# Routers by maxima of eight, late norms and paired heads in stage 2, C products on VectorE or GpSimd, and one new order of an eight-stage network

## The reference, cut to what matters

```
0  L0_attn  LN, in_proj, 2 convs, silu, dt/B/C, softplus, 16-state scan over 256 steps, gate, LN, MLP
1  L0_ffn   RMS, attention (16 heads), RMS, 7 routed experts (sigmoid, top 2) + 1 shared
2  L1_attn  linear attention, 4 heads of 64, a prefix sum over 512 tokens
3  L1_ffn   MLP with binarized weights
4  L2_attn  causal attention, 16 heads over 128 columns
5  L2_ffn   8 experts, top 2 of the logits, softmax of the two, gelu
6  L3_attn  causal attention, 16 heads of 64, keys pruned by a ranking
7  L3_ffn   8 experts, softmax, top 2, weights over their sum + 1e-20, + 2 shared
```

```
scan:     h = dA_t * h + dBu_t ; y_t[d] = sum_n h[d, n] * C_t[n]
stage 2:  p = elu(x) + 1 ; q, k = p / (norm(p) + 1e-6)
          y = (q . cumsum(k v^T)) / (q . cumsum(k) + 1e-6)
routers:  scores, idx = top_k(probs, 2) ; weights dense over the experts
```

## Time and profile before

| | |
|---|---|
| runs | 1410.33, 1411.71, 1419.28 us; median 1411.71 |
| profiled execution, first to last instruction | 1417.1 us |
| PE busy | 1334.4 us (94%), 8752 records |
| PEld busy | 930.4 us (66%) |
| DVE busy | 1016.5 us (72%), 3744 instructions |
| ACT busy | 899.3 us (63%), 2493 |
| POOL busy | 711.3 us (50%), 707 |
| mean granted clock | 0.950 |
| DMA | 65.8 MB, mean 46 GB/s |

### The profile page before, as it was taken

The page is one execution under the profiler, slowest core; times in us unless marked ns, Lnnn a source line. Parts: engine busy times, 40 slices in busy tenths (PEclk is TensorE's granted clock), DMA queues, the critical chain, the costliest instruction groups (busy, mean ns, idle before and its releaser), DMA issues. The chain is left out here.

```text
span 1417.1 us, 26200 instructions
## 1 busy us (share of the span) xinstructions
PE 1334.4 (94%) x8752; PEld 930.4 (66%) x8752; DVE 1016.5 (72%) x3744; ACT 899.3 (63%) x2493; POOL 711.3 (50%) x707
## 2 busy tenths in 40 slices
PE   8778789999969999999999999999999999999997
PEld 4224455667535687677777777777888877776665
DVE  5989889794687556758687874393598998745334
ACT  6636888876633676775877776466577668744231
POOL 2736475864462655455365554638343425432543
PEclk9668999998987979999999999999999999999999
DMA  8541000001150100110010002210200002003330
GB/s 281 157 118 30 1 2 30 25 2 54 29 150 1 66 2 1 54 63 1 1 61 2 1 2 73 110 60 1 79 2 2 1 2 90 2 1 90 90 97 23
DMA packets 21278, 65.80 MB, mean 46 GB/s; under 512 B 1852, under 2 KB 8252, under 8 KB 18840
## 3 DMA queue, kind: packets, MB, share of 16 engines
q1 hardware_dynamic: 21144, 64.12, 14.2%
HBM read 61.83 MB, written 2.29 MB: 45 GB/s over the span
## 5 line engine op out<-in xcount | busy, mean ns | idle before, releaser
L1371 ACT ACTIVATE arena<-arena 128x256 f32<-128x256 f32 (+3 forms) x792 | 347.5, 442 | 52.7 <-DVE arena L1858 27.2
L1371 ACT ACTIVATE arena<-bank 128x512 f32<-128x512 f32 (+3 forms) x365 | 198.0, 570 | 258.4 <-PE bank L923 132.5
L923 PE MATMUL bank<-XT,W 128*128 128x512 f32 (+1 forms) x752 | 292.6, 524 | 0.0
L2224 POOL TENSOR_TENSOR arena<-arena 128x256 f32<-128x256 f32 x192 | 119.1, 620 | 305.8 <-DVE arena L1873 305.4
L923 PEld LDWEIGHTS bank<-W,arena 128*128 128x128 f32 x1888 | 231.9, 194 | 48.7 <-issue 38.1
L923 PE MATMUL bank<-arena 128*32 128x128 f32 (+8 forms) x2912 | 247.4, 342 | 8.5 <-DVE arena L1879 2.7
L923 PE MATMUL bank<-W,arena 128*128 128x128 f32 (+1 forms) x1888 | 244.5, 280 | 6.7 <-DVE arena L1623 3.2
L2180 POOL TENSOR_TENSOR arena<-arena 128x512 f32<-128x512 f32 (+1 forms) x108 | 171.0, 1604 | 151.6 <-DVE arena L1617 90.7
L923 PEld LDWEIGHTS bank<-arena 128*32 128x32 f32 (+4 forms) x2912 | 165.4, 157 | 89.9 <-issue 57.7
L923 PE MATMUL bank<-arena,W 128*128 128x512 f32 (+3 forms) x412 | 183.7, 684 | 25.6 <-DVE arena L1794 13.3
L927 PE MATMUL bank<-CF,arena 128*128 128x128 f32 x1312 | 186.7, 282 | 21.3 <-POOL arena L2225 6.5
(11 more groups left out here) (128 smaller groups left out, 1697.9 us busy)
## 6 DMA issues: line engine op xcount, KB each, us to landing
arena<-rws SPq DMA_DIRECT2D x8, 2048.0 KB, 7.6
arena<-rep SPq DMA_DIRECT2D x62, 256.0 KB, 5.0
arena<-rws SPq DMA_DIRECT2D x4, 1792.0 KB, 6.6
W<-w SPq DMA_DIRECT2D x2, 2124.0 KB, 8.1
arena<-rws SPq DMA_DIRECT2D x8, 384.0 KB, 10.3
W<-w SPq DMA_DIRECT2D x1, 2692.0 KB, 10.1
W<-w SPq DMA_DIRECT2D x1, 2256.5 KB, 9.0
W<-w SPq DMA_DIRECT2D x1, 2002.5 KB, 16.1
```

The lines of the kernel that those rows point to most:

```text
L923: return e.matmul(o, lhsT, rhs, start=start, stop=stop, skip_group_check=True)
L1371: return e.activation(o, a, func, **kw)
L2224: e.tensor_tensor(px[:, :, 0:128], px[:, :, 0:128], rec[:, :, 0:1].to_broadcast([128, 2, 128]), ALU.mult)
```

## The change

- **C products** leave the scan. `0.bc` now also copies C from its bank to SBUF (ACT), so that bank is free at once. A new step `0.hc` (64 of them) multiplies the scanned 128x512 by it on whichever of DVE and POOL the planner picks: 32 come to DVE, 32 to POOL. `0.ac` waits for four of them.
- **Stage 2, late norms.** exp(min(x, 0)) is made by ACT in two operations, Relu(-x) and Exp(-that), so DVE keeps one operation of 512 columns per `2.t` where it had three. q and k are transposed without the norm. A new step `2.r` makes the norms beside it: k's goes into v and its 65th column (POOL, 4x64 columns), q's multiplies the 1e-6 in `2.y`.
- **Stage 2, pairs.** `2.h` makes two heads at once, one on partitions 0 to 63 and one on 64 to 127, into two banks: 16 pairs in place of 32 single heads.
- **Routers.** Eight columns everywhere (7 + one of -1). The top two come from DVE's maximum of eight (`e.max`) and `match_replace`, each four times per router on 8 columns. Weights lie at strides of 32 columns, so stages 1 and 7 need one full transpose (128 columns) instead of four narrow ones; stage 5 has four full ones. `ew` of stages 1 and 7 is four small DMAs instead of one.
- **4.ex**: the 128 small operations go from DVE to POOL.
- **6.s** reads all 128 partitions; those of 64 up are scaled to zero in q (`half`), so it is a full matmul.
- **The planner** knows the array's division of each step (`TILED`), adds 0.09 or 0.16 us to its plan where it changes, and prefers to stay (`STAY`). `PARTS`, `AHEAD`, `URGENT` and `HASTE` have new numbers, so the order is new on every engine.

Over both programs, counted in the order in which the instructions stand: PE has 5108 matmuls before and 5084 now, and the array's division changes 439 times before and 352 now. Of stretches that follow a full-array one, 197 became 139. Of those, 120 and 84 stand behind the end of chunk 3's stage 0, the last stage 0 of all.

The diff, cut to its core (`0.hc` stands in it twice, on DVE and on POOL):

```diff
-    "0.bc": "P1.77 A.51"
-    "0.st": "V1.90"
-    "2.t": "P1.38 A.79 V1.25 G1.10 V.63 G1.62 V1.19"
+    "0.bc": "P1.73 A1.12"
+    "0.st": "V1.33", "0.hc": "V.72|G1.30"
+    "2.t": "P1.31 A1.52 V.71", "2.r": "G1.08 V.68 G1.64 V.62 G.62"
...
-HELD = {("0.bc", 0): [("c", 0, ("0.ac", 3, 0), 1, 1)], ...
+HELD = {...
+TILED = {"0.da": "r", "0.rb": "r", "1.sc": "r", ... "2.h": "q", "6.ex": "q", "6.pv": "d"}
+STAY = {"stay": 1507.00, "act": 0.91}
...
+            add("0.hc", q, ("0.st", q))
...
-                other = 1 if g == "A" and TABLE.get(x.name, table) != table else 0
-                key = (t + other * 0.5 - HASTE.get(x.name, 0.0), -x.tail - AHEAD...
+                other = STAY["act"] if g == "A" and TABLE.get(x.name, table) != table else 0.0
+                turn = STAY["stay"] if g == "P" and tiled(x) != tiles else 0.0
+                key = (t - HASTE.get(x.name, 0.0) + other, -x.tail - AHEAD... + turn)
...
-                    on.wait_ge(*filled(cc))
-                    on.wait_ge(*own.last())
-                    on.wait_ge(*emptied(a))
-                    tt(h, h, bank[cc.i][:, :], ALU.mult).then_inc(has["hc"], 1)
+                elif name == "0.hc":
+                    on.wait_ge(*emptied(u("c", "0.bc", c)))
+                    on.wait_ge(*own.last())
+                    on.wait_ge(*emptied(decays0(c, n)))
+                    tt(ring0(c, n), ring0(c, n), s0(c, 16), ALU.mult).then_inc(has["hc_v"], 1)
...
+                elif name == "0.hc":
+                    on.wait_ge(*emptied(u("c", "0.bc", c)))
+                    on.wait_ge(*emptied(decays0(c, n)))
+                    e.tensor_tensor(ring0(c, n), ring0(c, n), s0(c, 16), ALU.mult).then_inc(has["hc_g"], 1)
...
-                    r, t0 = slice(64 * (h % 2), 64 * (h % 2) + 64), bb * 256
-                    mm(ps[:, 0:256], kT[:, t0:t0 + 128], qT[:, t0:t0 + 256])
-                    mm(ps[:, 256:384], kT[:, t0 + 128:t0 + 256], qT[:, t0 + 128:t0 + 256]).then_inc(full[b.i], 1)
+                    for lo, hi, k, q in ((0, 256, t0, t0), (256, 384, t0 + 128, t0 + 128)):
+                        for i, b in enumerate(two):
+                            r = slice(64 * i, 64 * i + 64)
+                            ins = mm(bank[b.i][:, lo:hi], s2qk(c)[r, 2 + x, k:k + 128], s2qk(c)[r, x, q:q + hi - lo], lo == 0, True)
...
-                    own(ts(ex, ex, 1.0, None, ALU.min))
-                    stt(px, bank[b.i][:, :], 0.0, ex, ALU.max, ALU.add).then_inc(done[b.i], 1)
+                    stt(wk[:, 512:1024], bank[b.i][:, :], 0.0, wk[:, 0:512], ALU.max, ALU.add).then_inc(done[b.i], 1)
...
-                    tt(p3, p3, sm[:, 24:32].unsqueeze(2).to_broadcast([128, 8, 64]), ALU.mult).then_inc(has["pn2"], 1)
+                    e.reciprocal(v2(c)[:, n * 4:(n + 1) * 4, 64:65], norms2(c, n)[:, 4:8].unsqueeze(2)).then_inc(has["sn"], 1)
...
-                    mm(ps[:, 0:128], q0[0:64, t0:t0 + 128], k0[0:64, t0:t0 + 128])
+                    mm(ps[:, 0:128], q0[:, t0:t0 + 128], k0[:, t0:t0 + 128])
...
+                        for j in range(4):
+                            e.dma_start(w[:, j * 128:(j + 1) * 128], turned(s, c)[32 * j:32 * j + 8, :]).then_inc(d_ew[c], 16)
...
+            def largest(vals, m8):
+                for j in range(4):
+                    own(e.max(m8[:, j, :], vals[:, j, :]))
+            def take_two(o, vals, m8):
+                own(e.memset(m8[:, :, 2:8], TAKEN))
+                for j in range(4):
+                    own(e.match_replace(o[:, j, :], m8[:, j, :], vals[:, j, :], TAKEN))
```

More of the change, by code:

```diff
@@ L163, with emits @@
 }
-KINDS = sorted({k for e in EMITS.values() for k in e} | {"km_a", "km_v", "dA"})
-def emits(name, n):
+KINDS = sorted({k for e in EMITS.values() for k in e} | {"km_a", "km_v", "dA", "hc_v", "hc_g"})
+def emits(name, n, g):
+    if name == "0.hc":
+        return {"hc_v" if g == "V" else "hc_g": (0, 1)}
     if name == "1.km":
@@ L487, in order_of_steps @@
             table = TABLE[x.name]
+        more = 0.0
+        if g == "P":
+            if tiled(x) != tiles:
+                more = 0.16 if t < free[g] + 0.1 else 0.09
+            elif t > free[g] + 0.1:
+                more = 0.09
+            tiles = tiled(x)
         for role, last, fulls, gives in opened(x):
@@ L496, in order_of_steps @@
         order[g].append((x.name, x.s, x.c, x.n, p))
-        end = t + x.parts[x.at][1]
+        end = t + x.parts[x.at][1] + more
         free[g] = end
@@ L1013, in _ @@
                     for j in range(4):
-                        on.wait_ge(*after("hc", "0.st", c, 4 * n + j))
+                        kind = "hc_v" if ("hc_v", "0.hc", c, 4 * n + j) in counts else "hc_g"
+                        on.wait_ge(*after(kind, "0.hc", c, 4 * n + j))
                     for j in range(4):
@@ L1149, in _ @@
                     b, ps = first(name, c)
-                    k = 7 if s == 1 else 8
                     if s == 1:
@@ L1446, in _ @@
                 elif name == "0.bc":
-                    b = u("b", name, c)
-                    evict(b, s0(c, 8), bank[b.i][:, :])
+                    for k, to in (("b", s0(c, 8)), ("c", s0(c, 16))):
+                        b = u(k, name, c)
+                        evict(b, to, bank[b.i][:, :])
                 elif name == "0.f":
@@ L2050, in _ @@
                     on.wait_ge(*own.last())
-                    own(reduce(sm[:, 128:132], v3(lg), ALU.max))
-                    on.wait_ge(*own.last())
-                    tt(v3(wt_), v3(lg), sm[:, 128:132].unsqueeze(2).to_broadcast([128, 4, 8]), ALU.subtract).then_inc(has["rt_v"], 1)
+                    largest(lg, m8)
+                    top = m8[:, :, 0:1].to_broadcast([128, 4, 8])
+                    own(tt(wt_, lg, top, ALU.subtract))
+                    tt(e8, m8, top, ALU.subtract).then_inc(has["rt_v"], 1)
@@ L2054, in _ @@
                 elif name == "5.r":
-                    sm = s3(c, 0)
-                    lg, wt_ = sm[:, 0:32], sm[:, 32:64]
-                    kp = top_two(v3(lg), 8, [s3(c, 1)[:, 0:256], s3(c, 1)[:, 256:512], sm[:, 64:96], sm[:, 96:128]])
+                    wt_, e8, lg, m8 = (slot(5, c, k) for k in range(4))
+                    on.wait_ge(*after("rt_v", name, c))
+                    take_two(lg, lg, m8)
                     on.wait_ge(*after("rt_a", name, c))
-                    own(tt(wt_, wt_, kp, ALU.mult))
@@ L2060, in _ @@
-                    on.wait_ge(*own.last())
-                    shares(wt_, sm[:, 132:140], 8).then_inc(has["rt_w"], 1)
+                    scaled(wt_, s3(c, 0)[:, 128:136], e8[:, :, 0:2])
+                    kept(wt_, lg, wt_).then_inc(has["rt_w"], 1)
                 elif name == "7.r" and p == 0:
-                    b, sm = u("b", name, c), s3(c, 0)
-                    lg, wt_ = sm[:, 0:32], sm[:, 32:64]
+                    b, top = u("b", name, c), s3(c, 0)[:, 128:132]
+                    wt_, pr, lg, m8 = (slot(7, c, k) for k in range(4))
@@ L2218, in _ @@
                     e.memset(vz(s, c), 0.0).then_inc(has["vz"], 1)
+                elif name == "4.ex":
+                    unit, h = n // 2, n % 2
+                    bb, m = unit_of(4, unit)
+                    n2 = small(4, c, unit)[:, 4 * h:4 * h + 4].rearrange("p (j i) -> p j i", i=2)
+                    r = row4(c)[:, bb * 32:bb * 32 + 32].rearrange("p (i j r) -> p j i r", i=2, j=4)[:, 2 * h:2 * h + 2, :, m]
+                    on.wait_ge(*emptied(u("b", "4.r", c)))
+                    for j in range(2):
+                        on.wait_ge(*emptied(u(f"S{j}", name, c, n)))
+                    own(e.tensor_tensor(n2, n2, r, ALU.subtract))
+                    on.wait_ge(*own.last())
+                    e.tensor_tensor(n2, n2, r, ALU.add).then_inc(has["nm"], 1)
                 elif name in ("1.nm", "4.nm", "6.nm"):
```

254 lines of the change are left out of this document (130 added, 124 removed), and 154 rows, old and new, of tables (AHEAD, EMITS, HASTE, OPENS).

## The result

The changed kernel takes 1401.25 us (four executions, 1400.25 to 1402.29), against 1411.95 for the kernel before: a ratio of 0.9916, with an interval of 0.9887 to 0.9946. It is 10.7 us faster: clear of no change by that interval, but less than the 1% (14 us) that the prediction named. The forecast was 33 us faster, at 1378.

The account below looks back on a forecast made before the run. DVE mostly bounds the front, PE's work the rest. From 1417.1 us, 12.4 (rest), 14 (DVE's work) and 7 (C's bank) leave 1383.7; less 5.4 for the profiled execution, 1378 us, own range 1366 to 1390, whole range 1348 to 1405.

Parts of the forecast that it names:

- Two parts, two limits: Cut at the end of chunk 3's stage 0: a front that DVE mostly sets, and a rest that PE sets.
- The rest, -12.4: Behind the cut: less PE work from entries, exits, pairs and transposes, -12.4 us, counted in full.
- the term for pairs: Stage 2 behind the cut: a pair takes the same 0.66 us as one head, so 5.2 us go.
- entries, exits and transposes: PE behind the cut: fewer entries to divided arrays 3.3 us, fewer exits 2.3, fewer router transposes 1.6.
- PE busy all through: Sign for the rest: about 926 us from the cut to the end, without idle time of PE.
- DVE's price of a product, 1.18: Front: each of DVE's 32 C products with two SBUF operands takes 1.18 us, so DVE wins 6.4 of 44.
- C's bank, -7: Front: the bank C held through scans is free, saving a quarter of PE's 27.5 us of waits, -7 us.
- Stage 2, -9: Front: two operations leave DVE in each of 8 tiles, 1.41 us a tile; four fifths shorten the front, -9 us.
- 17.7 us of DVE at 0.79, and nothing for POOL: Front: DVE loses 17.7 us of work, 0.79 of it counts, -14 us; POOL's 41 us of products count nothing.
- The still front: Rival, chance 0.18: DVE and POOL shut each other out, POOL's queue takes back DVE's gain; 1399 us.
- that rival: Rival, chance 0.10: POOL becomes the front's limit, decisive at 0.9 busy and more; slower, 1420 to 1440 us.
- The greater gain: Rival, chance 0.25: the new order feeds PE in the front, a third of 69 us idle goes; 1357 us.

Follow-up runs that it names:

- e10: The changed kernel, planned without the price for a change of TensorE's array division: 1446.8 us.
- e1: The changed kernel, with DVE's 32 C products reading the decay's bank, into which their scans write, so one operand is in PSUM: 1395.1 us.
- e6: As e5 (old order), with C's bank given back when ACT has copied it, order and assignment of banks kept: 1415.7 us.
- e13: The kernel before in its own order, two DVE operations left out of each stage 2 tile (minimum with 1, product with the norms): 1401.1 us.
- e16: e14 and e13 together, in the old order: products split without the lock, stage 2 shorter on DVE: 1415.7 us.
- e3: The kernel before, with C also copied to SBUF by ACT and DVE's 64 products reading it there, C's bank kept as long: 1428.8 us.
- e5: As e3, but scans write into the decay's bank and the products read that bank and C from SBUF: 1415.7 us.
- e14: The kernel before in its own order, C in SBUF: 32 products on DVE reading the decay's bank, 32 moved to POOL: 1424.1 us.
- e15: As e14, but DVE's products read two SBUF operands (the ring and C): 1428.0 us.
- e2: The changed kernel with all 64 C products on DVE in e1's form, none on POOL: 1408.8 us.
- e7: The changed kernel with the two heads of each stage-2 pair issued one after the other on TensorE: 1401.3 us.

## Why the prediction was wrong, step by step

- **Two parts, two limits: right.** Wherever the order was kept, the front moved and the rest stayed (936.7 to 940.2 us in the old order, 927.3 to 930.8 in the new).
- **The rest, -12.4: near, in part by luck.** It is 10.6 us shorter (939.3 to 928.7 by the same reading). Three things make that up. PE's busy time fell by 16.6 us; about 4 of these are work that now runs ahead of the cut, which leaves 12.5 for the 12.4 of the sum; and PE's idle time rose by 6. The last two were not forecast and nearly cancel. Within the sum, the term for pairs was too high (3.3 for 5.2), so the others brought more than was forecast; entries, exits and transposes were not separated by a run. "PE busy all through" is a property of a fitted order: e10 has all but the same work and 44 us more.
- **DVE's price of a product, 1.18: nearly right.** With the 8 other operations of the group at their 0.97 of e1, the 32 products took (48.8 - 7.8) / 32 = 1.28 us. The 0.6 in it is POOL's busy share before; with 0.88, its share after, the same formula gives 1.40. Missing was POOL's side: its B products went from 1312 to 1432 ns. Together this is worth 6.1 us (e1).
- **C's bank, -7: wrong.** It is 0 with order and banks kept (e6). A wait of PE for DVE need not be a wait for a bank; the share of a quarter had no row behind it.
- **Stage 2, -9: right.** 7.4 and 8.4 us (e13, e16).
- **17.7 us of DVE at 0.79, and nothing for POOL: the step that failed.** The front was to end 21 us earlier and ends where it did. The factor comes near where work only leaves DVE or comes to it in the old order (0.7 in e3 against e5, 0.65 in e13); in the new order e1 gives 0.3. A product that moves to POOL is another matter. It takes 1.3 instead of 0.7 in the chain of its chunk, and it puts a wait for a scan into POOL's queue, ahead of other chunks' B products. In the old order 22 us fewer on DVE made the kernel 8 us slower (e14 against e5). The prediction named this queue and wrote "I count nothing". For products and bank together it had -5 and -7; in the old order the split with the lock costs 18 us (e15, 1428.0 against 1410.4). Where the work goes has to be priced like where it leaves.
- **The new order: not counted at all.** In the old order all the front's parts with the lock come to 1428.0 (e15) - 8.4 (stage 2) = 1419.6, and with the rest's 10.6 off to 1409; the changed kernel has 1401. So about 8 us are the order's, worked out and not run. It is an order for a split front: there the split gains 13.7 (e2 to e1), in the old one it loses 8. What in the new order makes the difference stays open, beyond that POOL stands 12.9 us at its C products there and 48.2 in e14.
- **The rivals.** The still front, given 0.18, is what happened: 1399 forecast, 1401 measured. Of its two reasons the shutting out is shown in the changed kernel itself (6.1 us, e1); POOL's queue takes back what DVE gives in the old order (e14), while in the changed kernel the split as a whole gains. POOL at 0.88 between 50 and 200 us stayed just under the 0.9 that was called decisive; e14 is slower by as much as that rival had it, at 1424, but in the old order and with POOL at 104.5 of 150 us. The greater gain did not come: PE stands for 471.0 - 398.6 = 72.4 us of the front, 69.3 before. Its sum had a slip as well, a third of 69 us being 23, not 21. The Trainium skill's rule of the exclusive lock (SBUF — State Buffer, section on the two separate sides) agrees with e1, e3 and e5. With the lock "always paid" DVE would have lost 4 us on the products, 3 us in the front at 0.79, where 5 were taken as gained: nearer to the result as a sum, though the price measured (1.28) lies between.

The profiled execution of before may have misled too, though not in the sum: by the estimate above its front was some 8 us longer than a middling one, and the 27.5 us that the bank's term was drawn from may hold part of that.

## What to carry to other kernels

Price a moved operation on both sides: its longer duration in its own chain, and everything that stands behind its wait in the queue that it joins. If two elementwise engines must both work on SBUF data, let one of them keep one operand in PSUM; writing a scan's result into the bank that it read cost the scan nothing to speak of (686 against 679 ns in e1), though the bank comes back one product later, and e1, the change with only this added, is the fastest kernel of all at 1395.1 us. And where a planner sets the order by fitted numbers, a change of parts cannot be judged by the order that it happens to come with: one planned price was worth 45 to 100 us here, more than all parts together.

## What was not expected of the hardware

- TensorE overlaps matmuls on different row halves that stand one behind the other in its queue: eight records take 0.86 us, as four take 0.85, whether their matmuls alternate or not (changed kernel, e7).
- A POOL operation is drawn out as well when it meets DVE's operations with two SBUF operands: 1432 ns on average against 1298 when DVE reads a bank (changed kernel, e1).
- A scan that writes over the bank it reads takes about as long as one that writes to SBUF (e1, first halves of the two kinds, 686 and 679 ns):
```profile
L1911 DVE TENSOR_TENSOR_SCAN bank<-bank,arena 128x256 f32<-128x256 f32 x32 | 22.0, 686 | 6.9 <-ACT bank L1483 6.9
L1917 DVE TENSOR_TENSOR_SCAN arena<-bank,arena 128x256 f32<-128x256 f32 x32 | 21.7, 679 | 5.9 <-ACT bank L1483 5.6 <-POOL arena L2285 0.2
```
